# Router products of three feed-forwards as float16 high and low parts, issued pair of tiles by pair

## The chip, the cores and the metric

The kernel runs on one core of one Trainium2 chip. The metric is the device time of one execution in microseconds, as the median over several executions. TensorE multiplies, VectorE and ScalarE move and transform data between PSUM and SBUF, GpSimd (POOL) does gate products and powers, and SyncE (SP) issues the transfers.

## The reference

A residual stream `x` of 4 x 256 tokens with 256 features passes four layers. Each adds a cross-attention and then a feed-forward, both on the layer-normalised stream. The feed-forwards of layers 1, 2 and 3 are mixtures of experts, and each begins with a router: a product of all 1024 tokens with a narrow matrix, from which gates per token come.

```python
# feed-forward 1: 64 experts, 8 chosen, one shared expert with a gate of its own
logits = jnp.dot(h, router_w.T)
probs = jax.nn.softmax(logits.astype(jnp.float32), axis=-1)
top_vals, top_idx = lax.top_k(probs, TOP_K)
shared = jax.nn.sigmoid(jnp.dot(h, shared_expert_gate_w.T)) * shared
# feed-forward 2: self-attention first, then 8 experts, 2 chosen, one shared
h = _rms(x, w_ln2).reshape(B * S, H)
logits = h @ w_router
probs = jax.nn.softmax(logits, axis=-1)
top_w, top_i = jax.lax.top_k(probs, TOP_K)
# feed-forward 3: 16 experts, 4 chosen
logits = jnp.einsum('ed,btd->bte', gate_w, x)
scores = jax.nn.sigmoid(logits) + gate_b
weights, indices = jax.lax.top_k(scores, TOP_K)
```

The router matrices have 65, 9 and 16 columns, the shared expert's gate included. The choice of experts must come out as in fp32, so the logits need nearly fp32's precision.

## The kernel before, in words

The 1024 tokens are 8 tiles of 128 on the partitions (`NT = 8`); the 256 features are two halves when they stand on the partitions (`KT = 2`). The kernel is written engine by engine: every engine has its own list of instructions in program order, and semaphores tie them together. Nothing is scheduled by a planner, so the order of the code is the order of each queue.

Large products run in float16 with a split: a value times 64 (`SPLIT`) is rounded to a high part, the rest is a low part, and three products (high x high, high x low, low x high) stand for the fp32 one. `xh` and `xl` hold the two parts of the transposed tokens for the feed-forward, `up_w` and `dn_w` those of its weights.

Between an attention and its feed-forward lies a stretch that is called `pre` with its number here. In `pre1` and `pre3` it has these steps:

- VectorE finishes the layer norm into `xn` (`dve_ln`, L265), in `pre1` it also makes the low parts of the first two up weights (`dve_up_lo`, L1382).
- TensorE transposes `xn` tile by tile into PSUM banks 0 to 3, two tiles to a bank (`pe_transpose_tiles`, L277).
- ScalarE reads each bank (`act_parts`): for each feature half it writes an fp32 copy into `xT` (L1528) and the float16 high part into `xh` (L1530).
- VectorE writes the low parts (`dve_parts`, L1537) from the same bank and `xh`.
- TensorE computes the router products (`pe_logits`, L1551) in fp32 from `xT` and the router weights, 8 tiles x 2 halves, after all fp32 copies are there, into banks 4 and 5. Then it waits until all low parts are there (`gates`) and starts the feed-forward.

`pre2` has a whole self-attention in front; after it the tokens are normalised again (`z`, L2130), transposed, and taken through the same helpers with a scale per feature (the norm's weight).

The feed-forward (`pe_ffn`) works in steps `st`, each one half of the tokens times 128 hidden features: six gate products (L1303 to L1305, first with bank `h`), six up products into bank 2 (all twelve are called up products below), and from the eighth step on the down products (L1348 to L1350). VectorE handles the gates between the first steps (maximum, softmax, top experts), between its part of the feed-forward's first steps (`dve_front`, L1455, L1458 and L1462); ScalarE supplies `tanh` and copies (L1415, L1411).

In the trace a float16 matrix product is recorded as one weight load (PEld) and one product (PE). An fp32 product, the transposes aside, is recorded as two passes, each with its load: the 16 router products of a stretch are `x32` there.

## Time and profile before

| | |
|---|---|
| median of 3 runs | 1392.7 us (1391.67 to 1398.78) |
| the profiled execution | 1398.84 us |
| its span, first to last instruction | 1396.8 us |
| mean granted TensorE clock | 0.928 of full |
| busy: TensorE, its weight loads | 1235.4 us (88%), 826.4 us (59%) |
| busy: VectorE, ScalarE, GpSimd | 912.7, 502.8, 328.7 us |
| router products (L1551), 3 x 16 in 3 x 32 passes | 7.0 us (9 columns), 6.5 (65), 5.7 (16) |
| fp32 copies (L1528), 16 + 8 | 7.4 + 4.1 us |

Busy times overlap between engines, so only the chain of waits tells what sets the time. The granted clock is a share of 2.4 GHz and takes two values, 0.5 and 1; in a window that holds both, the mean is printed.

### The profile page before, as it was taken

The numbers are of one execution on the slowest core, as the hardware profiler recorded it, in microseconds if no ns is written. First come the engines' busy times: TensorE is split into PE (matmuls) and PEld (weight loads), VectorE is DVE, ScalarE is ACT, GpSimd is POOL, SyncE is SP. The second block draws the span as 40 slices with busy tenths as digits, with TensorE's granted clock in tenths as the row PEclk, the third lists the DMA queues.
The fourth block names the chain that finished last, engine by engine and source line by source line (L and its number), as shares of the span: only waits on it lengthen the run. The fifth ranks groups of instructions, "written<-read, shape, count | busy, mean of one in ns | idle before, by whom it ended". The sixth has DMA issues, their size and how long they took to land.

```text
span 1396.8 us, 21512 instructions
## 1 busy us (share of the span) xinstructions
PE 1235.4 (88%) x8348; PEld 826.4 (59%) x8348; DVE 912.7 (65%) x1737; ACT 502.8 (36%) x1141; POOL 328.7 (24%) x314
## 2 busy tenths in 40 slices
PE   5868869999879999999899678996999786899997
PEld 4654546999755666665567444664566554556665
DVE  4766656766737666666667595775666767566666
ACT  3322323011123333333353224652433342455553
POOL 0000030655502333333203320000333300033332
PEclk9878979999979999999899796997999988899999
DMA  3020043000034443444230000000343300043442
GB/s 134 2 80 8 23 141 119 1 2 1 1 145 111 109 127 112 121 118 115 90 131 1 0 15 1 2 1 0 116 124 117 96 16 1 33 127 108 132 126 76
DMA packets 41542, 97.16 MB, mean 70 GB/s; under 512 B 5447, under 2 KB 18247, under 8 KB 39393
## 3 DMA queue, kind: packets, MB, share of 16 engines
q1 hardware_dynamic: 41440, 95.79, 22.3%
q8 instruction: 66, 1.08, 0.3%
q14 instruction: 36, 0.29, 0.1%
HBM read 94.35 MB, written 1.42 MB: 69 GB/s over the span
## 4 chain that ended last, share of the span: by engine, by line
PE 76%; DVE 15%; ACT 4%; issue 2%; POOL 2%; DMA 1%; SPq 0%; DVEq 0%; POOLq 0%; ACTq 0%
PE PS L1303 9%; PE PS L1304 9%; PE PS L1305 9%; PE PS L1348 4%; PE PS L1349 4%; PE PS L1350 4%; PE PS L927 3%; PE PS L945 2%; PE PS L1109 2%; PE PS L1936 2%; PE PS L1953 2%; DVE arena L497 2%; PE PS L914 1%; PE PS L916 1%; PE PS L915 1%
## 5 line engine op out<-in xcount | busy, mean ns | idle before, releaser
L1518 POOL TENSOR_TENSOR arena<-arena,m_g 128x512 f32<-128x512 f32 x142 | 182.0, 1283 | 434.4 <-DMA m_g<-gate_rows 252.7
L1303 PE MATMUL PS<-arena 128*128 128x512 f16 x608 | 233.6, 384 | 5.1 <-DVE arena L1455 2.2
L1304 PE MATMUL PS<-arena 128*128 128x512 f16 x608 | 233.2, 384 | 0.0
L1305 PE MATMUL PS<-arena 128*128 128x512 f16 x608 | 233.0, 383 | 0.0
L1348 PE MATMUL PS<-arena 128*128 128x256 f16 x608 | 165.8, 273 | 9.0 <-DVE arena L1475 8.1
L1350 PE MATMUL PS<-arena 128*128 128x256 f16 x608 | 165.7, 273 | 0.0
L1349 PE MATMUL PS<-arena 128*128 128x256 f16 x608 | 165.7, 273 | 0.0
L1458 DVE SCALAR_TENSOR_TENSOR arena<-arena,PS 128x512 f32<-128x512 f32 x112 | 76.8, 686 | 128.1 <-ACT arena L1415 128.0
L1415 ACT ACTIVATE arena<-PS 128x512 f32<-128x512 f32 x112 | 66.9, 597 | 253.3 <-PE PS L1305 242.9
L1475 DVE TENSOR_TENSOR arena<-arena 128x512 f16<-128x512 f32 x142 | 111.7, 786 | 3.2 <-ACT arena L1425 3.2
L1305 PEld LDWEIGHTS PS<-arena 128*128 128x128 f16 x608 | 60.1, 99 | 73.6 <-issue 3.5
L1303 PEld LDWEIGHTS PS<-arena 128*128 128x128 f16 x608 | 60.5, 100 | 67.6 <-DVE arena L1455 3.2
L1425 ACT ACTIVATE arena<-arena 128x512 f16<-128x512 f32 x142 | 88.0, 620 | 22.0 <-PE PS L1350 19.9
L1304 PEld LDWEIGHTS PS<-arena 128*128 128x128 f16 x608 | 60.1, 99 | 59.5 <-issue 2.8
L991 POOL TENSOR_TENSOR arena<-arena 128x256 f32<-128x256 f32 x96 | 67.6, 726 | 106.2 <-DVE arena L1019 106.1
L1462 DVE TENSOR_TENSOR arena<-arena,PS 128x512 f32<-128x512 f32 x112 | 77.0, 687 | 16.7 <-PE PS L1305 2.5
L1348 PEld LDWEIGHTS PS<-arena 128*128 128x128 f16 x608 | 59.4, 98 | 37.2 <-issue 11.5
L270 POOL TENSOR_TENSOR rstd<-var_e,half_neg 128x8 f32<-128x8 f32 x8 | 13.1, 1638 | 257.7 <-DVE var_e L262 257.7
L1349 PEld LDWEIGHTS PS<-arena 128*128 128x128 f16 x608 | 59.5, 98 | 19.1
L1382 DVE SCALAR_TENSOR_TENSOR arena<-w_stage,arena 128x512 f16<-128x512 f32 x80 | 59.2, 742 | 7.7 <-ACT arena L1377 7.7
L1350 PEld LDWEIGHTS PS<-arena 128*128 128x128 f16 x608 | 59.5, 98 | 6.9
L2013 ACT ACTIVATE arena<-PS,arena 128x128 f32<-128x128 f32 (+1 forms) x128 | 52.0, 420 | 28.2 <-DVE arena L2027 27.8
(271 smaller groups left out, 2346.0 us busy)
## 6 DMA issues: line engine op xcount, KB each, us to landing
w_stage<-in_up SPq DMA_DIRECT2D x80, 256.0 KB, 2.9
m_g<-gate_rows SPq DMA_DIRECT2D x70, 256.0 KB, 4.2
arena<-in_heads SPq DMA_DIRECT2D x16, 1088.0 KB, 5.1
w_stage<-in_down SPq DMA_DIRECT2D x80, 128.0 KB, 4.1
m_g<-gate_rows SPq DMA_DIRECT2D x17, 512.0 KB, 4.0
m_g<-gate_rows SPq DMA_DIRECT2D x6, 448.0 KB, 4.4
m_g<-gate_rows SPq DMA_DIRECT2D x6, 384.0 KB, 4.3
m_g<-gate_rows SPq DMA_DIRECT2D x6, 320.0 KB, 4.1
```

Of the source, the lines that this page charges most:

```text
L991: ins = pool.tensor_tensor(r[:, f, :], r[:, f, :], p2[:, 1 - f, :], ALU.add)
L1303: pe.matmul(to, w_hi, x_hi, start=(k == 0), stop=False)
L1304: pe.matmul(to, w_lo, x_hi, start=False, stop=False)
L1305: ins = pe.matmul(to, w_hi, x_lo, start=False, stop=(k == KT - 1))
L1348: pe.matmul(to, h_hi, w_hi, start=(c == 0 and i % 2 == 0), stop=False)
L1349: pe.matmul(to, h_hi, w_lo, start=False, stop=False)
L1350: ins = pe.matmul(to, h_lo, w_hi, start=False, stop=False)
L1425: act.activation(hid_part(0, st % 2), m_c[:, st % 2, :], ACT.Copy).then_inc(s.hi, 1)
L1458: dve.scalar_tensor_tensor(a, t, 1.0, g_ps, ALU.add, ALU.mult).then_inc(s.a, 1)
L1462: dve.tensor_tensor(m_b[:, st % LAG, :], a, u_ps, ALU.mult).then_inc(s.prod, 1)
L1475: dve.tensor_tensor(hid_part(1, st % 2), m_c[:, st % 2, :], hid_part(0, st % 2), ALU.subtract).then_inc(s.lo, 1)
L1518: pool.tensor_tensor(m_c[:, st % 2, :], m_b[:, st % LAG, :], m_g[:, st // 2 % 2, st % 2, :], ALU.mult).then_inc(s.c, 1)
```

## The change

The router products of feed-forwards 1, 2 and 3 are computed from `xh` and `xl`, which exist for the feed-forward anyway, and from a high and a low float16 part of the router weights (`router_parts`, made by two VectorE operations in `dve_router`, L1545 and L1546 of the changed kernel). Each fp32 product becomes three float16 ones (L1559 to L1561): 48 products with 48 loads, instead of 16 products in 32 passes with 32 loads. The logits come out 4096 times as large, and the activations that read them get a scale of 1 / 4096. The fp32 copies are gone. The router products are issued pair of tiles by pair, each after the low parts of its pair (semaphore `low`, counted up once a pair), and the last of these waits also stands for the old wait for `gates`.

```diff
@@ -1518,38 +1518,47 @@
 
-        def act_parts(src_ready, before, done, scales, f32_scales=None, f32_done=None):
+        def act_parts(src_ready, before, done, scales):
 
             for j in range(NT // 2):
                 nc.scalar.wait_ge(src_ready, before + 2 * j + 2)
                 for k in range(KT):
                     ps = pair_ps(j)[:, k, :, :]
-                    if f32_scales is not None:
-                        nc.scalar.activation(xT[:, k, 2 * j:2 * j + 2, :], ps, ACT.Copy,
-                                             scale=f32_scales(k)).then_inc(f32_done, 1)
                     nc.scalar.activation(xh[:, k, 2 * j:2 * j + 2, :], ps, ACT.Copy, scale=scales(k)).then_inc(done, 1)
 
-        def dve_parts(high_done, scales):
+        def dve_parts(high_done, scales, low_done):
 
             for j in range(NT // 2):
                 nc.vector.wait_ge(high_done, KT * (j + 1))
                 for k in range(KT):
                     ins = nc.vector.scalar_tensor_tensor(xl[:, k, 2 * j:2 * j + 2, :], pair_ps(j)[:, k, :, :], scales(k),
                                                          xh[:, k, 2 * j:2 * j + 2, :], ALU.mult, ALU.subtract)
-            return ins
+                ins.then_inc(low_done, 1)
+
+        def router_parts(cols):
+
+            return [ffn_w[:, 1024 + a * 256:1280 + a * 256].bitcast(F16)[:, 0:KT * cols].rearrange("p (k c) -> p k c", k=KT) for a in range(2)]
+
+        def dve_router(me, s, w, cols, loads):
+            dve, (w_hi, w_lo) = nc.vector, router_parts(cols)
+            dve.wait_ge(s.w, 16 * loads)
+            me.link(dve, dve.tensor_scalar(w_hi, w, SPLIT, None, ALU.mult))
+            dve.scalar_tensor_tensor(w_lo, w, SPLIT, w_hi, ALU.mult, ALU.subtract)
 
         def plain_scale(k):
             return SPLIT
 
-        def pe_logits(s, w, cols, ready, count):
-
-            pe = nc.tensor
-            pe.wait_ge(s.w, 16)
-            pe.wait_ge(ready, count)
-            for i in range(NT):
-                for k in range(KT):
-                    ins = pe.matmul(PS[:, 4 + i // 4, (i % 4) * cols:(i % 4 + 1) * cols], xT[:, k, i, :], w[:, k, :],
-                                    start=(k == 0), stop=(k == KT - 1))
+        def pe_logits(s, cols):
+
+            pe, (w_hi, w_lo) = nc.tensor, router_parts(cols)
+            for j in range(NT // 2):
+                pe.wait_ge(s.low, j + 1)
+                for i in (2 * j, 2 * j + 1):
+                    to = PS[:, 4 + i // 4, (i % 4) * cols:(i % 4 + 1) * cols]
+                    for k in range(KT):
+                        pe.matmul(to, xh[:, k, i, :], w_hi[:, k, :], start=(i % 4 == 0 and k == 0), stop=False)
+                        pe.matmul(to, xh[:, k, i, :], w_lo[:, k, :], start=False, stop=False)
+                        ins = pe.matmul(to, xl[:, k, i, :], w_hi[:, k, :], start=False, stop=(i % 4 == 3 and k == KT - 1))
             ins.then_inc(s.logit, 1)
 
         def logits_ps(cols):
...
@@ -1696,11 +1705,10 @@
             x_ready(nc.sync, 2 * n + (1 if n == 1 else 0))
             nc.sync.dma_start(ffn_w[:, 0:cols], d[f"router{n}"]).then_inc(pre[n].w, 16)
 
-        def pe_pre1(n, w, cols):
+        def pe_pre1(n, cols):
             x_ready(nc.tensor, 2 * n + 1)
             pe_transpose_tiles(xn, ln.xn, (2 * n + 1) * NT, ln.xT_ps)
-            pe_logits(pre[n], w, cols, ln.xT, ln_xT_before[2 * n + 1] + NT)
-            nc.tensor.wait_ge(pre[n].gates, 1)
+            pe_logits(pre[n], cols)
 
         def act_pre1(n):
             act, s = nc.scalar, pre[n]
...
@@ -1708,12 +1716,12 @@
             if n == 1:
                 act_up_hi(n, 0)
                 act_up_hi(n, 1)
-            act_parts(ln.xT_ps, ln_T_before[2 * n + 1], s.h, plain_scale, lambda k: 1.0, ln.xT)
+            act_parts(ln.xT_ps, ln_T_before[2 * n + 1], s.h, plain_scale)
             if n == 1:
                 act_front(1, 0)
                 act.wait_ge(s.e, 1)
-                act.activation(pr1, pr1, ACT.Exp).then_inc(s.t, 1)
-                act.activation(tiles_of1(sig), logits_ps(E1 + 1)[:, :, :, E1], ACT.Tanh, scale=0.5).then_inc(s.t, 1)
+                act.activation(pr1, pr1, ACT.Exp, scale=UNSPLIT).then_inc(s.t, 1)
+                act.activation(tiles_of1(sig), logits_ps(E1 + 1)[:, :, :, E1], ACT.Tanh, scale=0.5 * UNSPLIT).then_inc(s.t, 1)
 
         def pool_pre1(n):
             x_ready(nc.gpsimd, 2 * n + 1)
...
@@ -1734,7 +1742,8 @@
             dve_ln(3)
             dve_up_lo(1, 0)
             dve_up_lo(1, 1)
-            dve_parts(s.h, plain_scale).then_inc(s.gates, 1)
+            dve_router(me, s, r1_w, E1 + 1, 1)
+            dve_parts(s.h, plain_scale, s.low)
             dve.wait_ge(s.logit, 1)
             logits = logits_ps(E1 + 1)[:, :, :, 0:E1]
             me.link(dve, dve.tensor_reduce(tiles_of1(row1), logits, AX.X, ALU.max))
...
@@ -1766,7 +1775,8 @@
         def dve_pre3():
             dve, s, me = nc.vector, pre[3], own["dve"]
             dve_ln(7)
-            dve_parts(s.h, plain_scale).then_inc(s.gates, 1)
+            dve_router(me, s, r3_w, E3, 1)
+            dve_parts(s.h, plain_scale, s.low)
             dve.wait_ge(s.logit, 1)
             me.link(dve, dve.memset(sc3[:, :, E3:E3 + 4], -1e30))
             dve.tensor_copy(tiles_of(lg3), logits_ps(E3)).then_inc(s.lg, 1)
...
@@ -2079,8 +2089,7 @@
             pe_qkv()
             pe_self()
             pe_transpose_tiles(z, s.z2, 0, s.z2T_ps)
-            pe_logits(s, r2_w, E2 + 1, s.f, NT)
-            pe.wait_ge(s.gates, 1)
+            pe_logits(s, E2 + 1)
 
         def act_pre2():
             act, s = nc.scalar, pre[2]
...
@@ -2095,10 +2104,10 @@
             act_up_hi(2, 1)
             act_qkv()
             act_self()
-            act_parts(s.z2T_ps, 0, s.h, lambda k: p2_n2s[:, k:k + 1], lambda k: p2_n2[:, k:k + 1], s.f)
+            act_parts(s.z2T_ps, 0, s.h, lambda k: p2_n2s[:, k:k + 1])
             act.wait_ge(s.e, 1)
-            act.activation(pr2[:, :, 0:E2], pr2[:, :, 0:E2], ACT.Exp).then_inc(s.t, 1)
-            act.activation(sig, lg2[:, :, E2], ACT.Tanh, scale=0.5).then_inc(s.t, 1)
+            act.activation(pr2[:, :, 0:E2], pr2[:, :, 0:E2], ACT.Exp, scale=UNSPLIT).then_inc(s.t, 1)
+            act.activation(sig, lg2[:, :, E2], ACT.Tanh, scale=0.5 * UNSPLIT).then_inc(s.t, 1)
 
         def pool_pre2():
             x_ready(nc.gpsimd, 5)
...
@@ -2116,6 +2125,7 @@
                 dve.tensor_scalar(z[:, i, :], xn[:, i, :], rms_r[:, i:i + 1], None, ALU.mult).then_inc(s.z, 1)
             dve.wait_ge(s.w, 48)
             me.link(dve, dve.tensor_scalar(p2_n2s, p2_n2, SPLIT, None, ALU.mult))
+            dve_router(me, s, r2_w, E2 + 1, 3)
             dve_up_lo(2, 0)
             dve_up_lo(2, 1)
             dve_qkv(me)
```

Feed-forward 0 only has its semaphore renamed. The copy in `pre2` of the norm's weight is untouched.

In the order of instructions the change shows as follows. TensorE ahead of feed-forward 1, before (`xT` are the fp32 copies, `arena` holds the weights, `xh` and `xl`; what stands in brackets are the semaphores waited for):

```order
L277 MATMUL PS<-ident,xn 128x128 [waits ln_xn]
L277 MATMUL PS<-ident,xn 128x128
L1551 MATMUL PS<-arena,xT 128x65 [waits ln_xT,pre1_w]
L1551 MATMUL PS<-arena,xT 128x65 x15
L1303 MATMUL PS<-arena 128x512 [waits ffn_up_lo,pre1_gates]
```

And now, of the first pair of tiles the first products, and the last ones of the fourth pair:

```order
L277 MATMUL PS<-ident,xn 128x128 [waits ln_xn]
L277 MATMUL PS<-ident,xn 128x128
L1559 MATMUL PS<-arena 128x65 [waits pre1_low]
L1560 MATMUL PS<-arena 128x65
L1561 MATMUL PS<-arena 128x65
...
L1560 MATMUL PS<-arena 128x65
L1561 MATMUL PS<-arena 128x65
L1303 MATMUL PS<-arena 128x512 [waits ffn_up_lo]
```

One wait for everything became four waits for `pre1_low`, in front of products 1, 13, 25 and 37 of 48, and the first gate product has no wait for low parts of its own. (`x15` with the row before it are the 16 fp32 products, 8 tiles x 2 halves.)

VectorE ahead of feed-forward 1, the piece of the difference without the rows that follow unchanged, before and now:

```order
L265 TENSOR_SCALAR xn<-x,meanvar,rstd 128x256 x7
L1382 SCALAR_TENSOR_TENSOR arena<-w_stage,arena 128x512 [waits ffn_up_hi] x2
L1537 SCALAR_TENSOR_TENSOR arena<-PS,arena 128x256 [waits pre1_h]
L1537 SCALAR_TENSOR_TENSOR arena<-PS,arena 128x256
...
L1740 TENSOR_REDUCE arena<-PS 128x8 [waits pre1_logit]
```

```order
L265 TENSOR_SCALAR xn<-x,meanvar,rstd 128x256 x7
L1382 SCALAR_TENSOR_TENSOR arena<-w_stage,arena 128x512 [waits ffn_up_hi] x2
L1545 TENSOR_SCALAR arena<-arena 128x130 [waits pre1_w]
L1546 SCALAR_TENSOR_TENSOR arena<-arena 128x130 [waits own_dve]
L1534 SCALAR_TENSOR_TENSOR arena<-PS,arena 128x256 [waits pre1_h]
L1534 SCALAR_TENSOR_TENSOR arena<-PS,arena 128x256
...
L1749 TENSOR_REDUCE arena<-PS 128x8 [waits pre1_logit]
```

The split of the router weights stands between the splits of the up weights and the first subtraction. In `pre3` it stands behind the layer norm in the same way. In `pre2` it stands far ahead, before the self-attention:

```order
L2125 TENSOR_SCALAR arena<-xn,rms_r 128x256 x7
L2127 TENSOR_SCALAR arena<-arena 128x2 [waits pre2_w]
L1545 TENSOR_SCALAR arena<-arena 128x18 [waits pre2_w,own_dve]
L1546 SCALAR_TENSOR_TENSOR arena<-arena 128x18 [waits own_dve]
L1382 SCALAR_TENSOR_TENSOR arena<-w_stage,arena 128x512 [waits ffn_up_hi] x2
L1888 TENSOR_TENSOR arena<-PS,arena 128x256 [waits pre2_qkv]
```

There nothing else moved.

## Rows read from the trace of the kernel before

**Rows 1.** The page's chain of waits: each engine's share of the span.
```profile
PE 76%; DVE 15%; ACT 4%; issue 2%; POOL 2%; DMA 1%; SPq 0%; DVEq 0%; POOLq 0%; ACTq 0%
```

**Rows 2.** Chain of waits around feed-forward 1: start us, us, what.
```profile
405.59 6.48 PE PS L1551 x32
...
418.23 0.61 ACT arena L1415
```

**Rows 3.** Timeline of the first stretch: start us, us, engine, line, operation, shapes, count [idle before].
```profile
400.07 3.27 PE L277 MATMUL PS<-ident,xn 128*128 128x128 f32 x16 [4.18 <-DVE xn L265]
...
402.10 1.29 DVE L1382 SCALAR_TENSOR_TENSOR arena<-w_stage,arena 128x512 f16<-128x512 f32 x2
...
403.30 2.11 DVE L1537 SCALAR_TENSOR_TENSOR arena<-PS,arena 128x256 f16<-128x256 f32 x6
...
411.87 0.63 PE L1303 MATMUL PS<-arena 128*128 128x512 f16 x1
...
412.30 0.15 PEld L1305 LDWEIGHTS PS<-arena 128*128 128x128 f16 x1 [0.28 <-issue]
```

**Rows 4.** Windows, same stretch: us, busy us of each engine (instructions), granted clock, DMA.
```profile
402.80:406.20 3.40, 1.14 (x11) 0.94 (x9) 3.05 (x9) 2.92 (x11) 0.00 (x0) 1.00 0.99 420
406.20:411.80 5.60, 5.60 (x29) 5.60 (x28) 0.31 (x1) 0.00 (x0) 0.00 (x0) 0.50 0.73 299
411.90:416.10 4.20, 4.20 (x11) 1.44 (x11) 2.07 (x3) 1.18 (x3) 0.00 (x0) 0.50 0.02 4
```

**Rows 5.** Timeline of the second stretch, before feed-forward 2.
```profile
952.69 3.45 PE L277 MATMUL PS<-ident,arena 128*128 128x128 f32 x16 [6.90 <-DVE arena L2130]
953.85 0.47 ACT L1528 ACTIVATE xT<-PS,arena 128x256 f32<-128x256 f32 x1 [9.70 <-PE PS L277]
...
956.90 0.88 DVE L1537 SCALAR_TENSOR_TENSOR arena<-PS,arena 128x256 f16<-128x256 f32 x2 [0.58 <-ACT arena L1530]
...
959.56 6.97 PE L1551 MATMUL PS<-arena,xT 128*128 128x9 f32 x32 [3.42 <-ACT xT L1528]
...
966.38 0.59 PE L1303 MATMUL PS<-arena 128*128 128x512 f16 x1
```

**Rows 6.** Windows of the second stretch.
```profile
955.80:959.15 3.35, 0.34 (x3) 0.10 (x1) 2.19 (x6) 3.35 (x10) 0.00 (x0) 1.00 0.01 2
959.20:969.40 10.20, 9.84 (x40) 7.94 (x41) 2.34 (x10) 1.21 (x5) 0.00 (x0) 0.50 0.00 0
```

**Rows 7.** Timeline of the third stretch, before feed-forward 3.
```profile
1187.69 3.65 PE L277 MATMUL PS<-ident,xn 128*128 128x128 f32 x16 [4.18 <-DVE xn L265]
...
1190.12 0.76 DVE L1537 SCALAR_TENSOR_TENSOR arena<-PS,arena 128x256 f16<-128x256 f32 x2 [0.31 <-ACT arena L1530]
...
1193.28 5.68 PE L1551 MATMUL PS<-arena,xT 128*128 128x16 f32 x32 [1.94 <-ACT xT L1528]
...
1198.80 0.59 PE L1303 MATMUL PS<-arena 128*128 128x512 f16 x1
```

**Rows 8.** Windows of the third stretch.
```profile
1191.30:1194.60 3.30, 1.36 (x13) 1.35 (x13) 2.20 (x6) 2.11 (x8) 0.00 (x0) 1.00 0.00 0
1194.70:1201.50 6.80, 6.80 (x28) 5.11 (x28) 0.90 (x4) 0.31 (x1) 0.00 (x0) 0.50 0.00 0
```

**Rows 9.** Timeline at full clock: fp32 transposes, small products of self-attention, an f16 load.
```profile
939.21 1.09 PE L1936 MATMUL PS<-ident,arena 128*128 128x128 f32 x8 [0.49 <-ACT arena L2013]
...
940.23 1.07 PE L1953 MATMUL PS<-arena 128*32 128x128 f32 x16
...
417.17 0.10 PEld L1303 LDWEIGHTS PS<-arena 128*128 128x128 f16 x1
```

**Rows 10.** The page's groups: f16 products of 256 columns, mean ns of one.
```profile
L1348 PE MATMUL PS<-arena 128*128 128x256 f16 x608 | 165.8, 273 | 9.0 <-DVE arena L1475 8.1
```

**Rows 11.** DMA issues around the first stretch: KB each, us to landing.
```profile
arena<-in_router SPq DMA_DIRECT2D x1, 65.0 KB, 1.8
```

**Rows 12.** Timeline before self-attention in feed-forward 2's part: VectorE's weight splits.
```profile
802.75 1.29 DVE L1382 SCALAR_TENSOR_TENSOR arena<-w_stage,arena 128x512 f16<-128x512 f32 x2 [2.83 <-ACT arena L1377]
```

More of the change, by code:

```diff
@@ L1619, in pe_pre0 @@
             pe_transpose_tiles(z, s.z2, 0, s.z2T_ps)
-            pe.wait_ge(s.gates, 1)
+            pe.wait_ge(s.low, NT // 2)
         def act_pre0():
@@ L1643, in pool_pre0 @@
             pool_pow(pre[0].ssq, 1, rms_r[:], rms_e[:], pre[0].rr)
-            nc.gpsimd.wait_ge(pre[0].gates, 1)
+            nc.gpsimd.wait_ge(pre[0].low, NT // 2)
         def dve_norm_ms(me, ready, r_done):
@@ L1785, in act_pre3 @@
             act.wait_ge(s.lg, 1)
-            act.activation(lg3, lg3, ACT.Tanh, scale=0.5).then_inc(s.t, 1)
+            act.activation(lg3, lg3, ACT.Tanh, scale=0.5 * UNSPLIT).then_inc(s.t, 1)
         E2 = 8
@@ L2130, in dve_pre2 @@
                 dve.tensor_scalar(z[:, i, :], xn[:, i, :], rms_r[:, i:i + 1], None, ALU.mult).then_inc(s.z2, 1)
-            dve_parts(s.h, lambda k: p2_n2s[:, k:k + 1]).then_inc(s.gates, 1)
+            dve_parts(s.h, lambda k: p2_n2s[:, k:k + 1], s.low)
             dve.wait_ge(s.logit, 1)
@@ L2185, in _ @@
             pe_latent(3)
-            pe_pre1(3, r3_w, E3)
+            pe_pre1(3, E3)
             pe_ffn(3)
```

15 lines of the change are left out of this document (7 added, 8 removed).

## The prediction

> **What bounds the kernel now.** I read the chain of waits first, because it tells which engine a microsecond must come from. TensorE carries 76% of it, VectorE 15% and ScalarE 4% [rows 1]. The places of the change are the three stretches between a transposed token block and the first up product of feed-forwards 1, 2 and 3. The chain of the first of them shows the whole problem in two rows: the 16 fp32 router products, recorded as two passes each (x32), stand in it as one piece of 6.48 us, and the chain comes back to ScalarE only at 418.23, after the first 18 products of the feed-forward [rows 2].
>
> The timeline of that stretch shows what is serial. The transposes run from 400.07 to 403.34; VectorE, after two weight splits that end at 403.39, takes 2.11 us for six subtractions (0.35 each). ScalarE meanwhile makes two copies of every quarter, and the router products start at 405.59, when the last fp32 copy is there [rows 2, 3]. All through them only TensorE works: the windows show 5.60 of 5.60 us busy there, with VectorE at 0.31 and ScalarE at 0 [rows 4]. The first up product starts at 411.87 [rows 3]. The second stretch has the same shape: transposes 952.69 to 956.14, ScalarE's first copy at 953.85, router products 959.56 for 6.97 us, first up product 966.38 [rows 5]. So has the third: transposes end at 1191.34, router products 1193.28 for 5.68 us, first up product 1198.80 [rows 7].
>
> The granted clock belongs to the reading. It was full (2.4 GHz) while TensorE idled before each router block, half (1.2 GHz) during nearly all of it, and still half until 416.1, 969.4 and 1201.5, that is for 4.2, 3.0 and 2.7 us of the dense up products behind it [rows 4, 6, 8]. The 32 passes take about 0.2 us each, whether they have 65, 9 or 16 columns.
>
> **What one new product costs.** No row shows an f16 product with few columns, so it is bounded. An fp32 pass costs (6.97 - 0.36) / 31 = 0.213 us with 9 columns at half clock [rows 5]; fp32 transposes of 128 columns cost (1.09 - 0.30) / 7 = 0.113 us at full clock [rows 9]. Columns from 9 to 128 hardly matter: the load of 128 weight columns sets the pace, and it follows the clock. An f16 load is recorded with 0.15 us at half and 0.10 us at full clock [rows 3, 9]; the difference of 0.05 us is what 128 columns differ by between 1.2 and 2.4 GHz if each takes one cycle, and 0.213 us is two cycles for each in an fp32 pass. So I take half of the fp32 pace, **0.107 us at half clock and 0.056 us at full clock**. From below: a pair of load and product is issued every (1.07 - 0.29) / 15 = 0.052 us [rows 9], so 0.052 is the floor that rows show. From above: an f16 product of 256 columns is recorded with 273 ns from start to end [rows 10]; if products did not overlap at all, each would cost that. The value is nearest to the halved fp32 pace since it is the same array doing the same load.
>
> The 48 new products replace 32 passes. At half clock they take 48 x 0.107 = 5.1 us against 6.5 to 7, at full clock 2.7 us. That alone is small. The larger part is where they lie: pair of tiles by pair, beside VectorE's subtractions, which before ran for nobody's benefit while TensorE waited and worked after them.
>
> A rule speaks against the full-clock price. The Trainium skill, page "TensorE: Matmul & The Clock Gate", section "LDWEIGHTS (loading the stationary operand)", gives a load of P columns as P / 1.2 ns, whatever the clock: 107 ns. The two records of rows 3 and 9 speak for a load that follows the clock. By the rule the sum below would be 9.7 us instead of 15.5.
>
> **Part by part.**
> - *ScalarE* loses 24 copies, 8 per stretch (0.38 to 0.57 us each, started 0.27 to 0.36 apart). With half the work it keeps up with the transposes: its last f16 high part comes some 0.7 to 0.9 us after the last transpose. It stops being what the router products wait for.
> - *VectorE* gains two small operations before its subtractions (split of 130, 18 or 32 weight columns). Each is less than a 256-column subtraction, so 2 x 0.35 = 0.7 us from above, 0.2 from below; I take 0.6 in all. In feed-forward 1 they stand on the path, since VectorE becomes the one that TensorE waits for. The router's load landed 1.8 us after its issue, and the issue stands ahead of the layer norm, so it is there in time [rows 11]. In feed-forward 2 they lie in an idle time of 2.83 us that VectorE had before its weight splits [rows 12] and cost nothing. In feed-forward 3 they begin in VectorE's idle 0.31 us before 1190.12 [rows 7] and delay the subtractions to 1190.4.
> - *The scale* 1 / 4096 moves into activations that are there anyway, and waits change their semaphore: nothing.
> - *Queued behind:* TensorE's new waits (one per pair) hold only the router products and then the up products, which waited for the last low part before too. The first up weights and the split of the router weights are done by then.
>
> *Feed-forward 1.* Subtractions start at 403.39 + 0.6 = 404.0. The first pair is out at 404.75, so TensorE starts at 404.85 (0.1 for the semaphore); the eighth ends at 404.0 + 8 x 0.35 + 0.05 = 406.85, and the last pair starts at 406.95. All at full clock: 406.95 + 12 x 0.056 = 407.6, 4.3 us before 411.87. All at half clock TensorE itself is the limit: 404.85 + 48 x 0.107 = 410.0, 1.9 us. With the clock as granted before (full to 406.2, then half): two pairs by 406.2, then 24 x 0.107, 408.8, **3.1 us**.
>
> *Feed-forward 2.* Subtractions cost 0.88 us a pair [rows 5]. The first high parts are out about 0.85 us after 953.85, so pairs start at 954.7 and every 0.8 us; the last is out at 958.0. TensorE starts when its transposes are through, 955.95. Full clock: 958.1 + 0.65 = 958.75, 7.6 us before 966.38. Half clock: 955.95 + 5.1 = 961.1, 5.3 us. The clock was full there from 955.8 to 959.15 [rows 6]: **7.6 us**.
>
> *Feed-forward 3.* Subtractions 1190.4 to 1193.3, last pair 1193.4, done 1194.05, 4.75 us before 1198.80. Half clock: 1191.2 + 5.1 = 1196.3, 2.45 us. The clock was full from 1191.3 to 1194.6 [rows 8]: **4.75 us**.
>
> *Sum:* 15.5 us as granted; 9.7 with every product at half clock, 16.7 with every one at full clock.
>
> *What is given back.* Behind the start nothing else changes, every engine's work follows the first up product; only the clock does not. The up products cost 0.427 us at half clock and 0.215 at full. Before, 9.9 us of them ran at half clock, which cost about 5 us. If the clock had stayed up, these 5 us would be won on top; if it rose so late that all 18 products of the first steps were slow in each of the three, 3 x 18 x 0.212 = 11.4 us, 6.4 more would be lost. TensorE's short products are no denser than the old ones, during which the clock stayed low, so I expect it low again at the start of the feed-forwards and lost time of the same size; since the products begin sooner after an idle stretch, I take 1.5 us more. 15.5 - 1.5 = **14.0 us** saved.
>
> The profiled execution took 1398.84 us (span 1396.8); it would take 1384.8. It lies 6 us above the median of the runs, 1392.7, so the forecast for the median is 1392.7 - 14.0 = 1378.7, rounded **1379 us**. The three runs shown spread over 7 us, so 0.5% (7 us) is about what can be told from no change.
>
> **The rivals.**
> 1. *The load doesn't follow the clock, or the clock stays low throughout*: every product costs 0.107 us, TensorE is the limit in all three stretches, 9.7 - 1.5 = 8.2 us, 1384.5. For it: the router block ran at half clock in all three. Against it: the records of the loads, and the full clock just before each block. 13%. (The Trainium skill's rule on LDWEIGHTS, on the page named above, is the first half of this rival.) If the up products are slow for longer too, 6 us and 1386.5 (within 0.5%): 4% more.
> 2. *The short products keep the clock up*: TensorE no longer idles for 1.9 to 3.4 us before them, so the drop does not come. 16.7 + 5 = 21.7 us, 1371. For it: after the fp32 transposes the clock was full each time. Against it: the fp32 router products, as dense, did not raise it. 9%.
> 3. *Slower: products into the same few columns don't overlap.* Six products in a row add into the same 65, 9 or 16 columns. If each waits for the one before, it costs up to 0.273 us [rows 10]: 404.85 + 48 x 0.273 = 418.0, 969.1 and 1204.3, that is 6.1 + 2.7 + 5.5 = 14.3 us more, 1407. It decides from (7.0 + 10.4 + 7.6) / 144 = 0.174 us a product. Against it: fp32 pairs add into the same 9 columns at 0.213 us a pass, the pace of the load, and up products into the same bank at their own pace. 4%.
> 4. *The start of the feed-forward isn't what counts*, because something else (gate rows, weights) sets when its first steps are through; 1392. The chain runs from router products straight into up products, so 3%.
>
> **The numbers.** The forecast (gain of 10 to 18 us) has 67%. The likeliest time is 1379. The range reaches from rival 2's side, 1373, to 1386, which takes in all of rival 1 but its last part, and the scatter of a median by 2 us; what lies outside is most of rivals 2, 3 and 4. Faster by over 0.5% (below 1385.7): forecast, rival 2 and four fifths of rival 1, 0.87. Within: 0.09. Slower: 0.04.
>
> **What would show it.** In the profile after: no row of the fp32 copies; 144 f16 products at 0.05 to 0.11 us start to start, waiting for VectorE in the first and third stretch; the idle of ScalarE and VectorE during the router block gone; first up products 3.1, 7.6 and 4.8 us sooner after their transposes (11.8, 13.7 and 11.1 us from the first transpose before, 8.7, 6.1 and 6.4 after). The prediction is wrong if the products are spaced over 0.12 us, or if VectorE's subtractions start later than the two splits explain, or if the sum of the three distances shrinks by 14 us and the span doesn't.

## The result and the profile after

The changed kernel takes **1371.3 us** as the median of its runs (1368.6 to 1381.3) against 1394.5 us of the kernel before in the same measurement: ratio 0.984, 95% interval 0.981 to 0.987. The forecast was 1379 us with a range of 1373 to 1386, so the direction was right and the gain was missed: 14 us forecast, 23 us measured, and the time lies below the range.

The page of the kernel after, first lines and the chain of waits, answers to [rows 1] and the table. TensorE's share of the chain fell by one point, ScalarE's by one, and VectorE's rose by one; each of these is at the edge of what two executions of one kernel differ by (TensorE has 76% again in after_again).

```profile
span 1369.8 us, 21584 instructions
PE 1213.8 (89%) x8396; PEld 808.7 (59%) x8396; DVE 909.8 (66%) x1743; ACT 495.7 (36%) x1117; POOL 329.9 (24%) x314
...
PE 75%; DVE 16%; ACT 3%; issue 2%; POOL 2%; DMA 1%; SPq 0%; DVEq 0%; POOLq 0%; ACTq 0%
```

Now the three stretches in the timeline of the kernel after, answering to [rows 3, 5, 7] (columns as there). First the stretch before feed-forward 1:

```profile
398.06 3.27 PE L277 MATMUL PS<-ident,xn 128*128 128x128 f32 x16 [4.19 <-DVE xn L265]
...
401.29 0.22 DVE L1545 TENSOR_SCALAR arena<-arena 128x130 f16<-128x130 f32 x1
401.54 0.29 DVE L1546 SCALAR_TENSOR_TENSOR arena<-arena 128x130 f16<-128x130 f32 x1
401.75 2.73 DVE L1534 SCALAR_TENSOR_TENSOR arena<-PS,arena 128x256 f16<-128x256 f32 x8
...
404.93 0.38 PE L1303 MATMUL PS<-arena 128*128 128x512 f16 x1
```

The stretch before feed-forward 2, the same view:

```profile
940.60 3.37 PE L277 MATMUL PS<-ident,arena 128*128 128x128 f32 x16 [6.90 <-DVE arena L2140]
...
942.62 3.36 DVE L1534 SCALAR_TENSOR_TENSOR arena<-PS,arena 128x256 f16<-128x256 f32 x8 [0.24 <-ACT arena L1527]
...
946.36 0.38 PE L1303 MATMUL PS<-arena 128*128 128x512 f16 x1
```

And the one before feed-forward 3:

```profile
1168.34 3.65 PE L277 MATMUL PS<-ident,xn 128*128 128x128 f32 x16 [4.17 <-DVE xn L265]
...
1170.69 2.79 DVE L1534 SCALAR_TENSOR_TENSOR arena<-PS,arena 128x256 f16<-128x256 f32 x8
...
1173.85 0.38 PE L1303 MATMUL PS<-arena 128*128 128x512 f16 x1
```

To compare, I take two distances in each stretch: from the first transpose to the first up product, and from there to TensorE's first long wait for VectorE inside the feed-forward (its "return"). In the timeline of the kernel before, the returns of feed-forwards 1, 2 and 3 are these rows:

```profile
423.54 0.39 PE L1303 MATMUL PS<-arena 128*128 128x512 f16 x1 [0.16 <-DVE arena L1462]
...
975.39 0.39 PE L1303 MATMUL PS<-arena 128*128 128x512 f16 x1 [0.88 <-DVE arena L1462]
...
1208.33 0.39 PE L1303 MATMUL PS<-arena 128*128 128x512 f16 x1 [1.56 <-DVE arena L1455]
```

In the timeline of the kernel after they are these:

```profile
414.31 0.39 PE L1303 MATMUL PS<-arena 128*128 128x512 f16 x1 [0.16 <-DVE arena L1462]
...
955.56 0.39 PE L1303 MATMUL PS<-arena 128*128 128x512 f16 x1 [0.89 <-DVE arena L1462]
...
1182.04 0.39 PE L1303 MATMUL PS<-arena 128*128 128x512 f16 x1 [1.56 <-DVE arena L1455]
```

| | to the first up product, us | from there to the return, us | both |
|---|---|---|---|
| before | 11.80 + 13.69 + 11.11 = 36.6 | 11.67 + 9.01 + 9.53 = 30.2 | 66.8 |
| after | 6.87 + 5.76 + 5.51 = 18.1 | 9.38 + 9.20 + 8.19 = 26.8 | 44.9 |
| gain | 18.5 | 3.4 | **21.9** |

These 21.9 us are the whole of the measured 23 within its interval. The spans of the two profiled executions differ by 27 us. The 5 us more lie outside the three stretches; the execution before was 6 us above the median known when the prediction was made.

Two things differ from what the prediction had. The products first. Two neighbours with 65 columns and two with 9, timeline of TensorE after:

```profile
402.60 0.20 PE L1560 MATMUL PS<-arena 128*128 128x65 f16 x1
402.63 0.19 PE L1561 MATMUL PS<-arena 128*128 128x65 f16 x1
...
943.83 0.17 PE L1560 MATMUL PS<-arena 128*128 128x9 f16 x1
943.86 0.17 PE L1561 MATMUL PS<-arena 128*128 128x9 f16 x1
```

In the mean such neighbours start 0.032 and 0.026 us apart; I had taken 0.056. Then the clock, in the windows after (columns as in [rows 4]): all three blocks of products run at full clock or nearly so (first, third and fifth window: 1.00, 1.00, 0.90), and so do the first steps of feed-forwards 1 and 3 (second and sixth). Only feed-forward 2 still starts with a stretch at half clock (fourth).

```profile
402.50:404.90 2.40, 1.98 (x48) 1.62 (x49) 1.99 (x7) 0.00 (x0) 0.00 (x0) 1.00 1.02 432
404.90:408.90 4.00, 4.00 (x26) 1.88 (x23) 3.13 (x8) 1.18 (x3) 0.00 (x0) 1.00 0.86 346
943.90:946.30 2.40, 1.52 (x47) 1.25 (x46) 2.08 (x6) 1.12 (x4) 0.00 (x0) 1.00 0.00 0
947.00:950.10 3.10, 3.10 (x9) 1.12 (x8) 1.76 (x6) 0.96 (x3) 0.00 (x0) 0.50 0.00 0
1171.80:1173.80 2.00, 1.55 (x48) 1.36 (x47) 1.67 (x5) 0.69 (x3) 0.00 (x0) 0.90 0.03 8
1173.85:1180.10 6.25, 6.25 (x35) 2.83 (x32) 4.13 (x32) 2.02 (x4) 0.00 (x0) 1.00 0.01 1
```

### The profile page after: what moved, and what is told of

Read it like the earlier page. It is cut to its first block, busy times and chain, and to the rows that moved or that the text cites. A ratio compares the mean times of both kernels' runs of the same rounds, so it can differ in the third digit from the quotient of the medians.

```text
span 1369.8 us, 21584 instructions
## 1 busy us (share of the span) xinstructions
PE 1213.8 (89%) x8396; PEld 808.7 (59%) x8396; DVE 909.8 (66%) x1743; ACT 495.7 (36%) x1117; POOL 329.9 (24%) x314
## 4 chain that ended last, share of the span: by engine, by line
PE 75%; DVE 16%; ACT 3%; issue 2%; POOL 2%; DMA 1%; SPq 0%; DVEq 0%; POOLq 0%; ACTq 0%
PE PS L1303 9%; PE PS L1305 9%; PE PS L1304 9%; PE PS L1348 4%; PE PS L1350 4%; PE PS L1349 4%; PE PS L927 3%; PE PS L945 2%; PE PS L1109 2%; PE PS L1946 2%; PE PS L1963 2%; PE PS L914 2%; PE PS L916 1%; PE PS L915 1%; PE PS L1928 1%
## 5 line engine op out<-in xcount | busy, mean ns | idle before, releaser
L1415 ACT ACTIVATE arena<-PS 128x512 f32<-128x512 f32 x112 | 66.8, 597 | 247.7 <-PE PS L1305 237.3
L1425 ACT ACTIVATE arena<-arena 128x512 f16<-128x512 f32 x142 | 88.0, 619 | 21.7 <-PE PS L1350 18.8
```

Source lines behind the costliest of these rows:

```text
L1425: act.activation(hid_part(0, st % 2), m_c[:, st % 2, :], ACT.Copy).then_inc(s.hi, 1)
```

## The experiments

Every ratio is to runs of the kernel before that were timed beside it on the same chip. The times of the kernel before spread from 1389.6 to 1407.3 us over all of them, so ratios are read and not times. Beside the ratio I give the sums of the two distances in the profiled execution, since they leave the rest of the kernel out: that rest, the span less the distances, lies between 1317.6 and 1332.1 us in the twelve profiled executions. Each row of distances is a single execution, and two of the same kernel (changed and after_again) differ by 1.3 us. The intervals of the ratios are some 4 us wide to each side, so a difference between two of these kernels of less than some 5 us can only be read from the distances.

| kernel | ratio (95%) | first distances | second | both |
|---|---|---|---|---|
| before | 1 | 36.6 | 30.2 | 66.8 |
| changed | 0.984 (0.981 to 0.987) | 18.1 | 26.8 | 44.9 |
| after_again | 0.982 (0.979 to 0.985) | 18.4 | 27.8 | 46.2 |
| f32_pairs | 0.988 (0.984 to 0.991) | 22.1 | 29.0 | 51.2 |
| f16_after_all | 0.988 (0.985 to 0.992) | 22.2 | 28.7 | 50.9 |
| keep_copies | 0.988 (0.984 to 0.992) | 22.4 | 30.4 | 52.9 |
| before_warm | 0.990 (0.987 to 0.994) | 30.1 | 28.3 | 58.3 |
| pause | 0.992 (0.989 to 0.996) | 33.0 | 28.5 | 61.4 |
| products_doubled | 0.984 (0.981 to 0.988) | 21.6 | 26.8 | 48.4 |
| hoist | 0.980 (0.977 to 0.982) | 17.3 | 26.6 | 43.9 |
| hoist_again | 0.978 (0.976 to 0.980) | 17.1 | 26.7 | 43.7 |
| hoist_warm | 0.977 (0.975 to 0.980) | 15.8 | 27.1 | 42.9 |

Theory A at first: the price of the products is the gain. Its rivals: B, the order (pair by pair, beside VectorE's work), and C, ScalarE's copies. After the first four runs a theory A2 was set beside them: the granted clock.

**after_again.** The changed kernel as it is.

> The changed kernel once more, so that the others of this call stand beside it on one chip. Every theory: 22 to 23 us below the kernel before (ratio 0.982 to 0.986), and from the first transpose to the first up product 6.9, 5.8 and 5.5 us as before.

0.982, as expected. In this execution the block before feed-forward 1 ran at half clock, as the windows show, and its products started 0.055 us apart. Against the execution above that cost 0.27 us up to the first up product and 1.2 us behind it.

```profile
400.00:402.00 2.00, 1.52 (x28) 1.53 (x29) 2.00 (x8) 0.31 (x2) 0.00 (x0) 0.50 0.99 422
402.00:404.50 2.50, 2.50 (x28) 1.67 (x26) 1.53 (x4) 0.00 (x0) 0.00 (x0) 0.50 1.00 425
```

**f32_pairs.** fp32 products and copies as before, only the wait changed:

```diff
-            pe.wait_ge(ready, count)
             for i in range(NT):
+                if i % 2 == 0:
+                    pe.wait_ge(ready, count - NT + KT * (i // 2 + 1))
```

> The kernel before, with fp32 products and fp32 copies, but each pair of tiles waits for its own copies alone. Theory A (the gain lies in the price of the products, 0.2 us a pass against 0.03 a product): TensorE is the limit at once, the passes start when the transposes end (1.9 to 3.4 us sooner) and take as long as before, so the first up products come 1.5 to 3.5 us sooner in each stretch, about 6 us in all (ratio 0.996). Theory B (the gain lies in the order, pair by pair beside VectorE's work): 12 us or more (ratio 0.991 or less).

17 us instead of 6: theory A's sum is too small, and B's number seems right. But the timeline shows that the earlier start is only half of it. The products start 8.2 us sooner after the transposes, summed over the three stretches. The 32 passes themselves are shorter too: from the first of them to the first up product it is 3.5, 5.1 and 3.7 us, where it was 6.3, 6.8 and 5.5 (6.3 us less in sum), and the second distances give 1.2 us. TensorE's timeline in the first stretch of f32_pairs:

```profile
398.46 3.27 PE L277 MATMUL PS<-ident,xn 128*128 128x128 f32 x16 [4.19 <-DVE xn L265]
...
401.57 3.68 PE L1552 MATMUL PS<-arena,xT 128*128 128x65 f32 x32
...
405.09 0.38 PE L1303 MATMUL PS<-arena 128*128 128x512 f16 x1
```

Its windows there, over the passes and over the first up products:

```profile
401.00:405.00 4.00, 4.00 (x38) 4.00 (x37) 3.56 (x10) 3.12 (x12) 0.00 (x0) 0.97 1.02 429
405.10:409.00 3.90, 3.90 (x21) 1.76 (x21) 3.06 (x8) 1.18 (x3) 0.00 (x0) 1.00 0.92 375
```

A pass costs 0.11 us here and 0.21 before [rows 3, 4, 5]; the granted clock was 0.97 against 0.50. Without TensorE's idle time of 1.9 to 3.4 us before them, the passes follow the transposes directly and run at full clock, in the second stretch until 3.3 us after the first of them. So the order gains twice, by the earlier start and by where it puts the block relative to the clock. The second part is theory A2, and I then tested it without any change of order.

**before_warm.** The kernel before with useless work added in that idle time:

```diff
+        def pe_fill(count):
+            for _ in range(count):
+                nc.tensor.matmul(PS[:, 6, :], ident_b[:], causal_b[:, 0:512], start=True, stop=True)
...
             pe.wait_ge(s.w, 16)
+            for j in range(NT // 2 - 1):
+                pe.wait_ge(ready, count - NT + KT * (j + 1))
+                pe_fill(3)
             pe.wait_ge(ready, count)
```

> The kernel before, with its order and its fp32 products and copies, but in the idle time between the transposes and the router products TensorE does 9 products of 128x512 bf16 (three after each of the first three pairs' copies) into a bank that nobody reads. Work is only added. Theory A2 (the granted clock is most of it: a pass costs 0.11 us at full clock and 0.2 us at half, and the first steps of the feed-forward are cheaper too): the clock stays full, the passes take 3.5 us instead of 5.7 to 7.0, together with the first steps 10 to 14 us less in all (ratio 0.990 to 0.993). Theory B (order and overlap): no gain, or up to 2 us more.

The kernel got faster by work that serves nothing: 13.6 us by the ratio (0.990; 0.0097 of 1399 us), with 9 to 18 us in its interval, and 8.5 us in the distances, which is also what the spans of the two profiled executions differ by. The timeline of the first stretch, TensorE:

```profile
402.38 3.64 PE L277 MATMUL PS<-ident,xn 128*128 128x128 f32 x16 [4.19 <-DVE xn L265]
406.25 2.99 PE L1546 MATMUL PS<-causal_b,ident_b 128*128 128x512 bf16 x8 [0.22 <-issue]
409.08 3.68 PE L1558 MATMUL PS<-arena,xT 128*128 128x65 f32 x32
412.60 0.38 PE L1303 MATMUL PS<-arena 128*128 128x512 f16 x1
```

The windows over part of the filling in the first stretch, and over the passes of all three:

```profile
406.30:408.40 2.10, 2.10 (x6) 0.70 (x6) 1.75 (x6) 1.73 (x7) 0.00 (x0) 0.50 1.04 439
409.10:412.50 3.40, 3.40 (x33) 3.40 (x32) 0.00 (x0) 0.00 (x0) 0.00 (x0) 1.00 0.98 400
958.30:961.40 3.10, 3.10 (x29) 3.10 (x29) 0.88 (x2) 0.25 (x1) 0.00 (x0) 1.00 0.00 0
1186.10:1189.60 3.50, 3.50 (x32) 3.50 (x33) 0.76 (x2) 0.16 (x1) 0.00 (x0) 1.00 0.02 5
```

The filling ends later than the last copy would have allowed (the passes start 1.0 us later in sum), and yet 3.68 us for the passes instead of 6.48 more than pays for it; over the three stretches the blocks are 7.5 us shorter. Behind the first of them the up products start 0.21 us apart at once, and the second distances are 2.0 us shorter in sum. Theory B expected nothing or a loss, so it can't be the whole: with order and products unchanged, the clock alone is worth 8.5 us in the stretches. What the clock is worth to the changed kernel, whose products are others, this run doesn't say.

**f16_after_all.** The changed kernel, all products behind the last low part:

```diff
-            for j in range(NT // 2):
-                pe.wait_ge(s.low, j + 1)
+            pe.wait_ge(s.low, NT // 2)
+            for j in range(NT // 2):
```

> The changed kernel, but all 48 products wait for the last low part. Theory A: 36 more products at 0.03 us stand behind the last low part in each stretch, 1.1 us each, 3.3 us in all, and up to 3 us more if the clock falls in the longer idle time. Theory B: most of the gain is lost, 10 us or more above the changed kernel.

The ratio is 0.006 above that of after_again, some 8 us (A's 3.3 to 6.3 is within its scatter), and the distances are 4.7 to 6.0 us longer. Two thirds of the gain or more stay without any overlap of products and subtractions, so B's "most is lost" is wrong too. The products start only 0.9 us sooner than the fp32 ones did (17.1 us after the first transposes in sum, against 18.0), and from there to the first up products it is 5.1 us instead of 18.6. So most of the gain lies in the price of the products, as theory A had it. The windows show what 48 products in a row cost: 2.5 us at half clock with 65 columns, 1.2 us at full clock with 9 or 16:

```profile
407.10:409.60 2.50, 2.50 (x48) 2.50 (x49) 0.00 (x0) 0.00 (x0) 0.00 (x0) 0.50 0.99 418
955.20:956.40 1.20, 1.20 (x48) 1.20 (x49) 0.00 (x0) 0.00 (x0) 0.00 (x0) 0.98 0.00 0
1183.20:1184.40 1.20, 1.19 (x47) 1.19 (x48) 0.00 (x0) 0.00 (x0) 0.00 (x0) 1.00 0.00 0
```

**keep_copies.** ScalarE still makes the fp32 copies:

```diff
                     ps = pair_ps(j)[:, k, :, :]
+                    if copies is not None:
+                        nc.scalar.activation(xT[:, k, 2 * j:2 * j + 2, :], ps, ACT.Copy, scale=copies(k))
                     nc.scalar.activation(xh[:, k, 2 * j:2 * j + 2, :], ps, ACT.Copy, scale=scales(k)).then_inc(done, 1)
```

> The changed kernel, but ScalarE still writes the 24 fp32 copies, which nobody reads. Theory A: ScalarE hands the high parts over as late as in the kernel before, which costs 0.3, 2.7 and 1.1 us in the three stretches, about 4 us in all. Theory C (the copies are what the gain comes from): 10 us or more.

The first distances are 4.0 us longer than in after_again, 0.0, 2.6 and 1.4, close to the 0.3, 2.7 and 1.1 worked out. The second distances are 2.7 us longer, since both later starts fell into a stretch at half clock. The ratio is 0.006 higher, 8 us. So the copies are worth 4 us directly and 6.7 with what follows. The distances stay below C's 10 us, which the ratio alone, uncertain by 7 us, would not exclude.

**pause.** 16 more copies by ScalarE (into `xT`, which nobody reads), and TensorE waits for them before its router products:

```diff
+        pause = ctx.enter_context(nc.semaphore("pause"))
...
+            if paused:
+                for m in range(16):
+                    if m == 8:
+                        ins.then_inc(pause, 1)
+                        nc.scalar.wait_ge(pause, 2 * [1, 2, 3].index(paused) + 1)
+                    ins = nc.scalar.activation(xT[:, m % 2, 2 * (m // 2 % 4):2 * (m // 2 % 4) + 2, :], xn[:, m % 8, :].rearrange("p (t c) -> p t c", t=2), ACT.Copy)
+                ins.then_inc(pause, 1)
...
             pe, (w_hi, w_lo) = nc.tensor, router_parts(cols)
+            pe.wait_ge(pause, 2 * pre.index(s))
```

> The changed kernel with a pause: ScalarE makes 16 more copies of 128x256 after its last high part, 4.5 us, and TensorE waits for them before its router products. Theory A2: the first up product comes some 4 us later in each stretch by the wait itself, and the idle time lets the clock fall to half, which adds the first steps at half clock, 1 to 2.5 us: 16 to 20 us in all above the changed kernel, of which 4 to 8 are more than the wait. It also shows the f16 products at half clock: 0.055 us or less if columns or issue bound them, 0.107 if the load of 128 weight columns does. Theory B: 12 us, the wait alone.

The products start 16.3 us later in sum than in after_again, counted from the transposes. By then all low parts are there, so the 48 products run without a wait between pairs, and the first up products come only 14.6 us later; the return comes 0.7 us later again. The ratio is 14 us above that of after_again. That is between B's 12 and A2's 16 to 20. A2's 4 to 8 us beyond the wait did not appear: the clock did fall, to half over all three blocks, but that costs the short products little, and the first steps of feed-forward 1 ran at half clock in after_again too. What the run shows best is the price of a product at half clock. Two neighbours in TensorE's timeline of pause, before feed-forward 2:

```profile
950.76 0.17 PE L1570 MATMUL PS<-arena 128*128 128x9 f16 x1
950.78 0.17 PE L1571 MATMUL PS<-arena 128*128 128x9 f16 x1
```

The windows over the products of the three stretches:

```profile
404.80:407.30 2.50, 2.50 (x47) 2.50 (x47) 0.00 (x0) 0.00 (x0) 0.00 (x0) 0.50 0.52 195
950.80:952.00 1.20, 1.20 (x48) 1.20 (x49) 0.00 (x0) 0.00 (x0) 0.00 (x0) 0.50 0.00 0
1179.50:1180.70 1.20, 1.20 (x47) 1.20 (x48) 0.00 (x0) 0.00 (x0) 0.00 (x0) 0.50 0.05 14
```

48 of them with 9 columns take 1.3 us at a granted clock of 0.50, 0.027 us each, nearly the same as at full clock (0.026). Loading 128 weight columns at one column a cycle would take 0.107 us there, so a load at that pace isn't what bounds them. From the first product to the first up product it is 5.2 us in sum over the three stretches, all at half clock, where the fp32 passes took 18.6, mostly at half clock.

**products_doubled.** As many products again, into a bank that nobody reads:

```diff
                     for k in range(KT):
+                        for _ in range(3):
+                            pe.matmul(PS[:, 6 + i // 4, (i % 4) * cols:(i % 4 + 1) * cols], xh[:, k, i, :], w_hi[:, k, :], start=True, stop=True)
```

> The changed kernel with each f16 router product followed by as many again into a bank that nobody reads, 96 instead of 48. If a product costs 0.03 us and is hidden but for the last pair's, 12 x 0.03 = 0.4 us per stretch, 1 us in all. If loads of 128 columns bounded them (0.056 us or more), 2 us or more.

0.984 against 0.982: unchanged within the intervals. The distances are 2.2 to 3.5 us longer. In the second and third stretch the first up product came 0.3 and 0.4 us later, as expected. In the first it came 2.5 us later, because the 96 products of 65 columns ran at half clock and took 5.1 us, more than VectorE's subtractions cover:

```profile
400.90:406.00 5.10, 5.09 (x95) 5.09 (x96) 1.94 (x6) 0.00 (x0) 0.00 (x0) 0.52 1.00 416
```

**hoist.** VectorE's splits moved into its idle time while GpSimd computes the power of the layer norm:

```diff
-        def dve_ln(m):
+        def dve_ln(m, meanwhile=()):
...
+            for f in meanwhile:
+                f()
             nc.vector.wait_ge(s.rstd, m + 1)
...
-            dve_ln(3)
-            dve_up_lo(1, 0)
-            dve_up_lo(1, 1)
-            dve_router(me, s, r1_w, E1 + 1, 1)
+            dve_ln(3, (lambda: dve_up_lo(1, 0), lambda: dve_up_lo(1, 1), lambda: dve_router(me, s, r1_w, E1 + 1, 1)))
...
-            dve_ln(7)
-            dve_router(me, s, r3_w, E3, 1)
+            dve_ln(7, (lambda: dve_router(me, s, r3_w, E3, 1),))
```

> The changed kernel, but VectorE splits the router weights (and, before feed-forward 1, the first two up weights) while it waits for GpSimd's power in the layer norm. Theory A2: the subtractions start 1.5 to 1.8 us sooner before feed-forward 1 and 0.3 us sooner before feed-forward 3, about 2 us below the changed kernel (ratio 0.981 against 0.9825). If VectorE isn't what TensorE waits for there: no difference.

> The kernel with VectorE's splits in the wait for GpSimd's power once more, to stand beside the next one: ratio 0.980 as before.

VectorE's timeline shows the splits in the gap that was 1.8 us and is 0.47 us now:

```profile
397.51 1.29 DVE L1384 SCALAR_TENSOR_TENSOR arena<-w_stage,arena 128x512 f16<-128x512 f32 x2
398.73 0.22 DVE L1547 TENSOR_SCALAR arena<-arena 128x130 f16<-128x130 f32 x1
398.98 0.29 DVE L1548 SCALAR_TENSOR_TENSOR arena<-arena 128x130 f16<-128x130 f32 x1
399.74 1.38 DVE L267 TENSOR_SCALAR xn<-x,meanvar,rstd 128x256 f32<-128x256 f32 x4 [0.47 <-POOL rstd L272]
```

The subtractions start 1.7 us sooner before feed-forward 1 and 0.3 us sooner before feed-forward 3, as expected. But the eight of them then take 3.0 to 3.1 us instead of 2.7 and 2.8, so only part arrives: the first up product of feed-forward 1 comes 5.9 to 6.0 us after the first transpose instead of 6.9 to 7.1, and that of feed-forward 3 0.0 to 0.1 us sooner. In the distances the two runs are 1.0 to 2.5 us below the two of the changed kernel. The ratios, 0.980 and 0.978 against 0.984 and 0.982, say 3 us or more; their intervals touch, so a gain is likely rather than certain, and the stretches account for no more than 2.5 us of it.

**hoist_warm.** TensorE filled up before the transposes as well (`pe_fill` as above):

```diff
             x_ready(nc.tensor, 2 * n + 1)
+            pe_fill(4)
+            nc.tensor.wait_ge(ln.var, 2 * n + 2)
+            pe_fill(6)
             pe_transpose_tiles(xn, ln.xn, (2 * n + 1) * NT, ln.xT_ps)
...
             pe_self()
+            pe.wait_ge(s.x2, NT)
+            pe_fill(12)
+            pe.wait_ge(s.ssq, 1)
+            pe_fill(6)
             pe_transpose_tiles(z, s.z2, 0, s.z2T_ps)
```

> The same with TensorE kept at work where it idles ahead of the transposes: 4 products of 128x512 bf16 after the attention's end and 6 after the variances (10 before feed-forwards 1 and 3; 12 and 6 before feed-forward 2's router), into a bank that nobody reads. Theory A2: the transposes run at full clock, where VectorE's layer norm paces them (2.7 us instead of 3.3), and the router products and first steps of the feed-forward at full clock too: 3 to 6 us less (ratio 0.976 to 0.978). Against it: if the idle products end late at half clock they delay the transposes by up to 1.5 us a stretch, and nothing is left.

The transposes ran at full clock and took 2.7 us instead of 3.3, as expected. TensorE's timeline of hoist_warm before feed-forward 1:

```profile
400.55 2.70 PE L279 MATMUL PS<-ident,xn 128*128 128x128 f32 x16 [1.07 <-DVE xn L267]
```

Its window over the transposes; over the block behind them the clock was full as well:

```profile
400.60:403.20 2.60, 2.60 (x16) 1.57 (x16) 2.60 (x9) 1.85 (x6) 0.00 (x0) 1.00 1.01 425
```

But the first distances gained only 1.3 us (15.8 against 17.1): before feed-forward 1 the chain runs from VectorE's layer norm straight into its subtractions. In feed-forward 2 the clock now stayed full and the second distance fell from 9.07 to 7.81; in feed-forward 3 it fell behind the products all the same (9.87 instead of 8.19). The ratio is 0.977 against 0.978: no difference, where 3 to 6 us were expected. The filling isn't worth its place here.

## Why the prediction was right and wrong

**What bounds the kernel** was read rightly: the three serial blocks of router products, each started by ScalarE's last copy, with the chain running straight into the up products. All of the gain was found in the stretches named, and rivals 3 and 4 did not occur. Products into the same few columns start 0.026 us apart, far below the 0.174 us from which rival 3 would have decided.

**The price of one product** is the first step that failed. The text said: "the load of 128 weight columns sets the pace, and it follows the clock", hence 0.056 us at full and 0.107 us at half clock, with 0.052 us as "the floor that rows show". Measured: 0.032 us (65 columns) and 0.026 us (9, 16) at full clock, 0.055 us (65) and 0.027 us (9, 16) at half. With 65 columns at half clock the price is that of the columns, 65 / 1.2 GHz = 0.054 us; with 9 it is nearly the same at both clocks, so nothing that follows the clock bounds it. The error was to carry an fp32 pace over to float16 by halving it, and to take the fastest row of this kernel, products with 128 fp32 columns, for a floor of all products. The recorded length of a load (0.10 and 0.15 us) was no price either: at 0.027 us apart the loads overlap.

The Trainium skill has part of this, in a section that I didn't weigh: "TensorE: Matmul & The Clock Gate", "Weight-path perf modes — Fast Weight Load (FWL) and DoubleRow", says that weights of 128 columns that are not fp32 are loaded by a faster path, split into four parallel chunks. 0.027 us at 1.2 GHz is 32 cycles, a quarter of 128, so the run `pause` agrees with a fourfold pace. The page gives the fourfold as theory for fp8 and about twofold as measured; twofold would be 0.053 us (an estimate from the page's figure), which the measurement contradicts. The same page, "Wait — 56ns, not 53.3ns?", names about 25 ns as the least distance of two products, and 0.026 us agrees. Its rule of P / 1.2 ns, which the prediction set against its own price, does not hold as the spacing of these loads; that it holds "whatever the clock" was the prediction's reading, since the formula names no clock.

**The sum for the blocks** came out as 15.5 us and was 18.5. With 0.03 us a product, its own arithmetic gives 407.3, 958.45 and 1193.8 for the three starts: 4.6, 7.9 and 5.0 us, 17.5 in all, against 4.9, 7.9 and 5.6 measured. So the price explains 2 of the 3 us, 1.2 of them in feed-forward 1, where 24 products had been put at 0.107 us. The last one is in the terms of VectorE: both splits took 0.51 us with 130 columns (0.22 and 0.29) and less with 32, where 0.6 was taken, and the subtractions followed 0.33 to 0.34 us apart before feed-forward 1, where 0.35 was.

**What is given back** is the step that failed by sign, and it cost the forecast the most: 4.9 of the 7.9 us by which the three stretches were missed. The text: "I expect it low again at the start of the feed-forwards and lost time of the same size; [...] I take 1.5 us more". Measured was a gain of 3.4 us: 11.67 to 9.38, 9.01 to 9.20, 9.53 to 8.19. In two of three cases the dense up products began while the clock was still full, and it stayed there; in feed-forward 2 it fell 0.6 us after they began. In after_again it stayed full in one of three, and the gain was 2.4 us. Rival 2 had the step right that the forecast had wrong: TensorE "no longer idles for 1.9 to 3.4 us" before the products (1.2 us before feed-forward 1, nothing before the others), "so the drop does not come". Its value, 21.7 us and 1371, is what was measured, but that is in part luck: 5 us were to come from the clock behind the blocks, where 3.4 did, and 16.7 from the blocks, where 18.5 did. Its other half, that the short products keep the clock up, stays open: they run for at most 2.5 us, in after_again the same products ran at half clock before feed-forward 1 behind 0.9 us of idle time, and no run here isolates their effect.

**The reason for the gain** was put down to the wrong part. Of the lower price of the products the text said "That alone is small", and "The larger part is where they lie [...] beside VectorE's subtractions". The runs show the reverse. In `pause` the float16 products are at half clock in all three stretches and run in one piece, and from the first of them to the first up product it is 5.2 us in sum, where the fp32 passes took 18.6: 13.4 us from the price, where the prediction's 0.107 us gave 3 to 4. The rest of the 21.9 us is the earlier start (6.8 us, less 1.8 since the products now wait for VectorE between pairs) and the 3.4 us behind the first up products. `f16_after_all` agrees: without overlap the distances lose 4.7 to 6.0 us, so the order is worth that much. The copies, by `keep_copies`, are worth 4.0 us of the first distances, since ScalarE hands over sooner without them.

The clock is the other thing left out. `before_warm` shows 8.5 us in the distances (13.6 by the ratio) from the clock alone, at unchanged order and price, and `f32_pairs` 17 us from a changed wait, about half of it by the clock (passes at 0.11 us instead of 0.21, and the first up products behind them). These gains don't add to the 13.4: a block can be made short by cheap products or by a full clock, and cheap ones hardly need it. The prediction had the numbers (half clock in all three blocks, full clock while TensorE idled before them; the third block was the shortest, 5.68 us, and its first 1.4 us were at full clock [rows 7, 8]) but treated the clock as given by the trace before, where it also depends on the idle time that the change removes. What float16 adds over `f32_pairs` is about 5 to 8 us (51.2 to 44.9 or 46.2 in the distances, 0.988 to 0.982 or 0.984 in the ratio).

**The range** reached down to 1373, since rival 2 was given 9% and left out. With the clock as a consequence of the change it would have been one of two even cases.

## What to carry to other kernels

Look at the granted clock of every short serial block on TensorE and at what TensorE did right before it: here fp32 blocks behind an idle time of 1.9 to 3.4 us took 5.5 to 6.8 us, and 3.5 to 4.0 us when the idle time was filled, and a change that closes such a gap can earn that on top of its own sum. It can't be counted on behind the block: the clock of the first up products differed between executions of the same kernel. Don't price a float16 product from an fp32 one: with few columns it cost a quarter to an eighth of an fp32 pass here, and the three products of a split are cheaper than the one in fp32. When a stretch is paced by a chain through three engines, look next for work in it that can move into an earlier wait, as VectorE's splits did.

## What the runs showed of the hardware

- Float16 products of 128 x 128 weights with 9 or 16 columns start 0.026 us apart at full (changed kernel) and 0.027 us at half clock (`pause`), each with its own load; with 65 columns 0.032 (changed kernel) and 0.055 us (after_again, `pause`).
- An fp32 pass with 9 to 65 columns costs 0.11 us at full (`before_warm`) and 0.21 us at half clock [rows 5], and each fp32 router product is two of them.
- 5.6 us of fp32 passes, with TensorE busy throughout, did not raise the clock [rows 4]. With nine products of 128x512 in the idle time ahead, the passes ran at 1.00 in all three stretches (`before_warm`); before feed-forward 1 the filling itself still ran at 0.50.
- With an idle time of some 6 us ahead of them, the router products ran at 0.50 in all three stretches (`pause`), where they ran at 1.00, 1.00 and 0.90 in the changed kernel. It also happens behind a short one: in after_again they ran at 0.50 before feed-forward 1 after 0.9 us, in the changed kernel's other execution at 1.00 after 1.2 us.
